# State space pipeline: four buffers for the copied C, and the spread of C as an own entry of TensorE's order

## The chip, the cores and the metric

One Trainium2 chip; the kernel runs on one of its cores. The metric is the device time of one execution in microseconds (us), taken as the median of several runs. Times inside a stage come from one profiled execution of the kernel before.

## What is computed

The program is a chain of eight residual layers on activations of 8 batches x 512 positions x 128 channels. The change touches the fifth layer alone, the state space layer. Its part of the reference, shortened:

```python
def _mamba_forward(x, W_in, conv_w, conv_b, W_x, w_dt, b_dt, A_log, D, W_out):
    xz = x @ W_in
    xc, z = jnp.split(xz, 2, axis=-1)
    ...                                     # causal convolution over 4 positions
    xs = jax.nn.silu(xconv)
    A = -jnp.exp(A_log)
    x_dbl = xs @ W_x
    Bp = x_dbl[..., 1:1 + D_STATE]
    Cp = x_dbl[..., 1 + D_STATE:]
    delta = jax.nn.softplus(d_raw * w_dt + b_dt)
    def step(h, inp):                       # over the positions
        dt, b, c, xt = inp
        At = jnp.exp(dt[..., None] * A)
        h = At * h + (dt * xt)[..., None] * b[:, None, :]
        y = jnp.einsum('bdn,bn->bd', h, c)
        return (h, y)
    ...
    y = (y + xs * D) * jax.nn.silu(z)
    return y @ W_out
```

There are 256 inner channels and 16 states (n). The layer's input is normalised first, and its output is added to the residual.

## The kernel before

The function is `mamba_all`. Channels lie on the 128 partitions in two chunks (c = 0, 1), positions run along the free dimension (512). One **step** k stands for one state n of one batch: k = 16 b + n, 128 steps in all. The recurrence over positions is one scan instruction of VectorE (DVE) per chunk, so a step is this pipeline:

- TensorE (PE) spreads row n of B over all partitions with one matmul into the PSUM bank `Bs` (L1571), and row n of C into the bank `Cs` (L1575). Both are in `spread(k)`, right behind each other. Each bank is single.
- DVE multiplies: u = dtx * Bs, both chunks in one instruction (L1384).
- ScalarE (ACT) copies `Cs` to one of the buffers `cs` (L1505) and computes the decay exp(dt * A) per chunk into the bank pair `A` (L1513).
- DVE scans per chunk: h (L1399), four buffers.
- GpSimd (POOL) weighs: hc = h * cs per chunk (L1468), six buffers.
- PE adds hc into the accumulators `Y` with an identity matmul per chunk (L1590).

The waits that matter: the copy of C for step k waits for the spread of C (`c_spread`) and for both weighings of step k - 2 (`weighed`), since `cs` has two buffers; the spread of C for step k waits until the copy of step k - 1 has read the bank (`c_taken`); the spread of B for step k waits for u of step k - 1 (`u_ready`).

```python
pe.matmul(Bs, ...).then_inc(S("b_spread"), 1)      # L1571
if k:
    pe.wait_ge(S("c_taken"), k)
pe.matmul(Cs, ...).then_inc(S("c_spread"), 1)      # L1575
```

Beside the steps of batch b, the five engines run the **batch work** of batch b + 1: normalisation (L1408 to L1523), transpose (L308), copy of it (`m_hT`, L1528), convolution and input projection (L1610, one group of four matmuls per chunk), the z part (L1616), `SiLU` on ACT (`m_xs`, `m_zs`, L1536), the projection for delta (L1621), |.| and relu on ACT (`m_mag` L1540, `m_pos` L1546), the projection to B and C (L1627), a split of them into three bf16 parts (L1553, L1421, L1561, L1562, L1442), softplus as a polynomial on DVE (L1428, L1431, L1439), dt * x on POOL (L1493). Behind a batch stand its closing pieces: D * x added (`m_yf`, L1450), the gate on POOL (L1496), the output projection (L1636) and the residual (L1455).

Every engine executes in program order. The order on an engine is made once, when the program is built: each piece of work is a Python generator that yields a due time ahead of its instructions, and `take_turns` always continues the generator whose due time is the smallest (ties go to the one listed first). Step k has the base time at(k) = 70 + 4 k, the batch work of b starts at at(16 b) - 58. These numbers set the order alone, they are no durations. Within one generator the order is that of its code, whatever due times it yields.

Of the kernel before, what the change touches and what calls it, by code (L numbers as in the profile page):

```python
# [18 lines left out]
ACT = mybir.ActivationFunctionType  # L19
AX = mybir.AxisListType  # L20

P = 128
B, T, C = 8, 512, 128
# [23 lines left out]
DI, DS, DC = 256, 16, 4  # L47
NCH = DI // P
# [106 lines left out]
def build(nc, x, pa, pb, pc, pk, pkb, b2, out):  # L155
    top = ExitStack()
    with top:
        def sb(ctx, name, shape, dt=F32):
            return ctx.enter_context(nc.sbuf_tensor(name, shape, dt))
# [1183 lines left out]
        def mamba_all(xres, wc, wconv, acoef):  # L1343
# [5 lines left out]
            with ExitStack() as ctx:  # L1349
                def room(name, shape, dt=F32):  # L1350
                    return sb(ctx, "m_" + name, shape, dt)
# [1 line left out]
                xs, zs, dt, dtx = (room(n, [P, 2, NCH, T]) for n in ("xs", "zs", "dt", "dtx"))  # L1353
                mag, pos, q = (room(n, [P, NCH, T]) for n in ("mag", "pos", "q"))
                u, h, hc = room("u", [P, 3, NCH, T]), room("h", [P, 4, T]), room("hc", [P, 6, T])
                cs, yf = room("cs", [P, 2, T]), room("yf", [P, NCH, T])
                hT, y = room("hT", [P, DC - 1 + T]), room("y", [P, NT, C])
                G, mid, rest = room("G", [96, 2, T], BF16), room("mid", [96, T], BF16), room("rest", [96, T])
                stats, mom, small = room("stats", [P, NT, 6]), room("mom", [P, 2, NT, 2]), room("small", [P, 2, 4, NT])
# [1 line left out]
                Y, Bs, Cs, A, X = flat[:, 0:2, :], flat[:, 2, :], flat[:, 3, :], flat[:, 4:6, :], flat[:, 6:8, :]  # L1361
# [3 lines left out]
                def S(name):  # L1365
                    if name not in used:
                        used[name] = pool[len(used)]
                    return used[name]

                def at(k):  # L1370
                    return 70.0 + STEP * k
# [87 lines left out]
                def gpsimd_scan(gp):  # L1459
                    for n in range(NCH * DS * B):  # L1460
                        k, c = divmod(n, NCH)
                        yield at(k) + 1.2 * (c + 2)
                        gp.wait_ge(S("scanned"), n + 1)
                        if c == 0:
                            gp.wait_ge(S("c_taken"), k + 1)
                        if n >= 6:
                            gp.wait_ge(S("summed"), n - 5)
                        gp.tensor_tensor(hc[:, n % 6, :], h[:, n % 4, :], cs[:, k % 2, :],  # L1468
                                         ALU.mult).then_inc(S("weighed"), 1)

                def gpsimd_batch(gp, b):
# [26 lines left out]
                def scalar_scan(act):  # L1498
                    for k in range(DS * B):
                        b = k // DS  # L1500
                        yield at(k) - 2.8
                        act.wait_ge(S("c_spread"), k + 1)
                        if k >= 2:
                            act.wait_ge(S("weighed"), NCH * (k - 1))
                        act.activation(cs[:, k % 2, :], Cs, ACT.Copy).then_inc(S("c_taken"), 1)  # L1505
                        for c in range(NCH):
                            yield at(k) + 1.2 * (c + 1) - 3.4
                            n = NCH * k + c
                            if k % DS == 0 and c == 0:
                                act.wait_ge(S("soft"), b + 1)  # L1510
                            if n >= 2:
                                act.wait_ge(S("scanned"), n - 1)
                            act.activation(A[:, c, :], dt[:, b % 2, c, :], ACT.Exp,  # L1513
                                           scale=acoef[:, c * DS + k % DS:c * DS + k % DS + 1]).then_inc(S("decayed"), 1)
# [47 lines left out]
                    act.activation(mid[64:96, :], rest[64:96, :], ACT.Copy).then_inc(S("mid_part"), 1)  # L1562

                def tensor_scan(pe):
                    def spread(k):
                        b, n = divmod(k, DS)
                        if n == 0:
                            pe.wait_ge(S("parted"), b + 1)
                        if k:
                            pe.wait_ge(S("u_ready"), k)  # L1570
                        pe.matmul(Bs, kb("sel32", 96)[:, n:n + 1].broadcast_to([96, P]), G[:, b % 2, :], start=True,  # L1571
                                  stop=True).then_inc(S("b_spread"), 1)
                        if k:
                            pe.wait_ge(S("c_taken"), k)
                        pe.matmul(Cs, kb("sel32", 96)[:, DS + n:DS + n + 1].broadcast_to([96, P]), G[:, b % 2, :],  # L1575
                                  start=True, stop=True).then_inc(S("c_spread"), 1)

                    for k in range(DS * B):
                        yield at(k) - 3.4
                        spread(k)  # L1580

                def tensor_sums(pe):
                    for k in range(DS * B):
# [56 lines left out]
                def all_lanes(name, eng):  # L1640
                    if name == "vector":
                        return [vector_scan(eng)] + [vector_batch(eng, b) for b in range(B)]
                    if name == "gpsimd":
                        return [gpsimd_scan(eng)] + [gpsimd_batch(eng, b) for b in range(B)]
                    if name == "scalar":
                        return [scalar_scan(eng)] + [scalar_batch(eng, b) for b in range(B)]
                    if name == "tensor":
                        return [tensor_scan(eng), tensor_sums(eng)] + [tensor_batch(eng, b) for b in range(B)]
                    return []
# [156 lines left out]
        with ExitStack() as ctx:  # L1806
# [28 lines left out]
            stage_block(load_all)  # L1835

            mamba_all(xres, wc, wc("convr"), acoef)

            with ExitStack() as inner:
# [158 lines left out]
```

## Time and profile before

| | us |
|---|---|
| median of 3 runs | 3947.56 (3946.97 to 3956.48) |
| the profiled execution, its own time | 3950.09 |
| its span in the trace | 3948.3 |
| the scan steps in it, first to last scan | 2145.7 to 2823.7 |
| granted clock of TensorE over the span, mean | 0.894 |

Times within the program are counted from the span's start. The granted clock of TensorE is given as a share of full speed: 1.00 is 2.4 GHz, 0.50 is 1.2 GHz.

### The profile page before, as it was taken

The numbers are of one execution on the slowest core, as the hardware profiler recorded it, in microseconds if no ns is written. First come the engines' busy times: TensorE is split into PE (matmuls) and PEld (weight loads), VectorE is DVE, ScalarE is ACT, GpSimd is POOL, SyncE is SP. The second block draws the span as 40 slices with busy tenths as digits, with TensorE's granted clock in tenths as the row PEclk, the third lists the DMA queues.
The fourth block names the chain that finished last, engine by engine and source line by source line (L and its number), as shares of the span: only waits on it lengthen the run. The fifth ranks groups of instructions, "written<-read, shape, count | busy, mean of one in ns | idle before, by whom it ended". The sixth has DMA issues, their size and how long they took to land. (4 is left out here: it accounts for less than half of the span.)

```text
span 3948.3 us, 49284 instructions
## 1 busy us (share of the span) xinstructions
PE 3142.3 (80%) x18104; PEld 1596.1 (40%) x18112; DVE 2337.4 (59%) x4715; ACT 1703.3 (43%) x3002; POOL 866.3 (22%) x920
## 2 busy tenths in 40 slices
PE   4988977748888397979784777767799996998977
PEld 1222224424444275656561222222377774222224
DVE  5777858856776234343423778888633234777754
ACT  1776741105556132323222454444433332576752
POOL 3222123422220000000001555555500001111001
PEclk9999987759999597989896888888899997899998
DMA  3101000001221100000002000000000000111100
GB/s 100 28 22 33 17 1 1 1 16 37 39 39 23 58 1 11 5 6 6 6 11 80 0 0 0 0 0 0 0 1 1 1 1 17 35 33 22 28 1 22
DMA packets 74519, 69.79 MB, mean 18 GB/s; under 512 B 10536, under 2 KB 72368, under 8 KB 72752
## 3 DMA queue, kind: packets, MB, share of 16 engines
q1 hardware_dynamic: 71216, 66.35, 7.3%
q8 instruction: 140, 2.29, 0.2%
q10 hardware_dynamic: 3072, 0.40, 0.1%
q14 instruction: 91, 0.75, 0.1%
HBM read 22.02 MB, written 6.29 MB: 7 GB/s over the span
## 5 line engine op out<-in xcount | busy, mean ns | idle before, releaser
L394 DVE TENSOR_REDUCE a_mx<-banks 128x1 f32<-128x512 f32 (+3 forms) x1536 | 870.7, 616 | 326.5 <-PE banks L654 200.9
L527 ACT ACTIVATE a_prob<-banks 128x512 f32<-128x512 f32 (+3 forms) x1536 | 776.0, 546 | 436.1 <-PE banks L677 206.6
L677 PE MATMUL banks<-a_Qs,a_Ks 64*128 64x512 bf16 (+3 forms) x1536 | 506.1, 363 | 108.3 <-ACT a_prob L527 101.0
L654 PE MATMUL banks<-a_Ks,a_Qs 63*128 63x512 bf16 (+3 forms) x1536 | 479.0, 370 | 28.0 <-DVE a_mx L394 15.6
L1590 PE MATMUL banks<-m_hc,kc 128*128 128x512 f32 x512 | 322.7, 735 | 124.0 <-POOL m_hc L1468 99.7
L1468 POOL TENSOR_TENSOR m_hc<-m_h,m_cs 128x512 f32<-128x512 f32 x256 | 326.6, 1294 | 305.9 <-DVE m_h L1399 305.9
L1104 ACT ACTIVATE b_room<-banks,w_b 128x512 f32<-128x512 f32 x256 | 176.0, 688 | 480.7 <-PE banks L1071 479.7
L703 PE MATMUL banks<-a_prob,a_vaug 128*32 128x512 f32 (+3 forms) x3072 | 376.3, 562 | 2.9 <-ACT a_prob L527 2.9
L1399 DVE TENSOR_TENSOR_SCAN m_h<-banks,m_u 128x512 f32<-128x512 f32 x256 | 300.7, 1207 | 27.5 <-ACT banks L1513 27.5
L654 PEld LDWEIGHTS banks<-a_Ks,a_Qs 63*128 63x128 bf16 x1536 | 130.6, 95 | 399.3 <-DVE a_mx L394 239.7
L677 PEld LDWEIGHTS banks<-a_Qs,a_Ks 64*128 64x128 bf16 x1536 | 132.2, 93 | 357.6 <-ACT a_prob L527 281.6
L1104 ACT ACTIVATE c_room<-banks 128x512 f32<-128x512 f32 x256 | 152.2, 597 | 272.9 <-PE banks L1071 272.8
L1071 PE MATMUL banks<-b_hT,w_b 128*128 128x512 f32 x512 | 256.6, 630 | 13.9 <-DMA b_x<-x 13.9
L1083 PEld LDWEIGHTS banks<-w_c,c_room 128*128 128x128 f32 x2048 | 245.6, 192 | 50.2 <-issue 50.0
L1513 ACT ACTIVATE banks<-m_dt,acoef 128x512 f32<-128x512 f32 x256 | 175.7, 690 | 196.9 <-DVE m_h L1399 192.8
L1083 PEld LDWEIGHTS banks<-w_b,b_room 128*128 128x128 f32 x2048 | 244.3, 194 | 35.0 <-issue 34.2
L1083 PE MATMUL banks<-w_c,c_room 128*128 128x128 f32 x2048 | 246.7, 275 | 0.0
L1083 PE MATMUL banks<-w_b,b_room 128*128 128x128 f32 x2048 | 246.7, 276 | 0.0
L1071 PE MATMUL banks<-c_hT,w_c 128*128 128x512 f32 x512 | 245.1, 605 | 1.2 <-ACT c_room L1104 1.2
L1384 DVE TENSOR_TENSOR m_u<-m_dtx,banks 128x1024 f32<-128x1024 f32 x128 | 154.7, 1208 | 99.4 <-PE banks L1571 96.7
L1590 PEld LDWEIGHTS banks<-m_hc,kc 128*128 128x128 f32 x512 | 96.0, 215 | 282.7 <-POOL m_hc L1468 221.5
L1118 DVE SCALAR_TENSOR_TENSOR c_room<-banks,c_room 128x128 f32<-128x128 f32 x224 | 63.0, 344 | 246.8 <-PE banks L1083 246.5
(322 smaller groups left out, 4400.9 us busy)
## 6 DMA issues: line engine op xcount, KB each, us to landing
a_Ks<-a_parts SPq DMA_DIRECT2D x288, 64.0 KB
a_Qs<-a_parts SPq DMA_DIRECT2D x288, 64.0 KB
w_c<-in_pc SPq DMA_DIRECT2D x5, 1024.0 KB
w_b<-in_pb SPq DMA_DIRECT2D x4, 1024.0 KB
a_Qs<-a_negm ACTq DMA_DIRECT2D x192, 2.0 KB
w_a<-in_pa SPq DMA_DIRECT2D x2, 1024.0 KB
xres<-in_x SPq DMA_DIRECT2D x8, 256.0 KB, 4.2
x<-xres SPq DMA_DIRECT2D x8, 256.0 KB
```

The lines of the kernel that those rows point to most:

```text
L394: dve.tensor_reduce(mx[:, g % 2, col:col + 1], M[:, k % 3, 0:keys[j]], AX.X, ALU.max).then_inc(S("max_read"), 1)
L527: act.activation(prob[:, n % 8, first_query[kt]:T], Sc[:, n % 2, first_query[kt]:T], ACT.Exp, scale=scale).then_inc(S("exped"), 1)
L654: i = pe.matmul(M[:, k % 3, 0:keys[j]], Qs[lo:lo + LAST, b % 4, pair, j * P:(j + 1) * P], Ks[lo:lo + LAST, b % 4, pair, 0:keys[j]], start= ...
L677: i = pe.matmul(Sc[:, n % 2, q0:T], Ks[lo:lo + HALF, b % 4, pair, kt * P:(kt + 1) * P], Qs[lo:lo + HALF, b % 4, pair, q0:T], start=True, s ...
L703: i = pe.matmul(V[32 * hl:32 * hl + 32, g % 2, q0:T], vaug[:, b % 3, kt, g % NG * GH + hl, :], prob[:, (4 * a + hl) % 8, q0:T], start=kt = ...
L1071: pe.matmul(bank[:, n % 2, :], w_up[:, n * P:(n + 1) * P], hT[:, :], start=True, stop=True).then_inc(S("up"), 1)
L1083: i = pe.matmul(bank[:, 2 + e % 2, j * P:(j + 1) * P], hbuf[:, n % 8, j * P:(j + 1) * P], w_down[:, n * P:(n + 1) * P], start=f == 0, stop ...
L1104: act.activation(hbuf[:, n % 8, :], bank[:, n % 2, :], func, bias=bias[:, n:n + 1] if bias is not None else 0.0).then_inc(S("acted"), 1)
L1399: dve.tensor_tensor_scan(h[:, n % 4, :], A[:, c, :], u[:, (k - 1) % 3, c, :], 0.0, ALU.mult, ALU.add).then_inc(S("scanned"), 1)
L1468: gp.tensor_tensor(hc[:, n % 6, :], h[:, n % 4, :], cs[:, k % 2, :], ALU.mult).then_inc(S("weighed"), 1)
L1513: act.activation(A[:, c, :], dt[:, b % 2, c, :], ACT.Exp, scale=acoef[:, c * DS + k % DS:c * DS + k % DS + 1]).then_inc(S("decayed"), 1)
L1590: pe.matmul(Y[:, c, :], ident, hc[:, (NCH * k + c) % 6, :], start=n == 0, stop=n == DS - 1, skip_group_check=True).then_inc(S("summed"), 1)
```

## The change

`cs` gets four buffers. The copy of C then waits for the weighings of step k - 4 in place of step k - 2. The copy's due time goes from at(k) - 2.8 to at(k) - 1.8. On TensorE the spread of B keeps at(k) - 3.4, and the spread of C gets an entry of its own at at(k) - 2.0. Lines behind this place are renumbered: the spreads are L1572 and L1577 in the changed kernel, and L1590, L1610, L1616, L1621, L1627, L1636 become L1588, L1608, L1614, L1619, L1625, L1634.

```diff
-                cs, yf = room("cs", [P, 2, T]), room("yf", [P, NCH, T])
+                cs, yf = room("cs", [P, 4, T]), room("yf", [P, NCH, T])
...
-                        gp.tensor_tensor(hc[:, n % 6, :], h[:, n % 4, :], cs[:, k % 2, :],
+                        gp.tensor_tensor(hc[:, n % 6, :], h[:, n % 4, :], cs[:, k % 4, :],
...
                 def scalar_scan(act):
                     for k in range(DS * B):
                         b = k // DS
-                        yield at(k) - 2.8
+                        yield at(k) - 1.8
                         act.wait_ge(S("c_spread"), k + 1)
-                        if k >= 2:
-                            act.wait_ge(S("weighed"), NCH * (k - 1))
-                        act.activation(cs[:, k % 2, :], Cs, ACT.Copy).then_inc(S("c_taken"), 1)
+                        if k >= 4:
+                            act.wait_ge(S("weighed"), NCH * (k - 3))
+                        act.activation(cs[:, k % 4, :], Cs, ACT.Copy).then_inc(S("c_taken"), 1)
...
                 def tensor_scan(pe):
-                    def spread(k):
+                    for k in range(DS * B):
                         b, n = divmod(k, DS)
+                        yield at(k) - 3.4
                         if n == 0:
                             pe.wait_ge(S("parted"), b + 1)
                         if k:
                             pe.wait_ge(S("u_ready"), k)
                         pe.matmul(Bs, ...).then_inc(S("b_spread"), 1)
+                        yield at(k) - 2.0
                         if k:
                             pe.wait_ge(S("c_taken"), k)
                         pe.matmul(Cs, ...).then_inc(S("c_spread"), 1)
-
-                    for k in range(DS * B):
-                        yield at(k) - 3.4
-                        spread(k)
```

What it moves. The instructions and their number are the same on every engine, and the orders of DVE and POOL are the same as before. Once per batch, seven times in all, TensorE's order changes at three places and ScalarE's at one.

The first place is on TensorE, beside the input projection of the next batch. Before (m_G is the split of B and C, m_hT the transposed input, m_hc the weighed states, m_xs the SiLU result):

```order
L1571 MATMUL banks<-m_G,kb 128x512
L1575 MATMUL banks<-m_G,kb 128x512
L1610 MATMUL banks<-m_hT,w_c 128x512 x4
L1590 MATMUL banks<-m_hc,kc 128x512 x2
L1571 MATMUL banks<-m_G,kb 128x512
L1575 MATMUL banks<-m_G,kb 128x512
L1616 MATMUL banks<-m_hT,w_c 128x512 x2
L1590 MATMUL banks<-m_hc,kc 128x512 x2
L1621 MATMUL banks<-m_xs,w_c 128x512 x2
```

The same stretch of TensorE in the changed kernel:

```order
L1572 MATMUL banks<-m_G,kb 128x512
L1608 MATMUL banks<-m_hT,w_c 128x512 x4
L1577 MATMUL banks<-m_G,kb 128x512
L1588 MATMUL banks<-m_hc,kc 128x512 x2
L1572 MATMUL banks<-m_G,kb 128x512
L1614 MATMUL banks<-m_hT,w_c 128x512
L1577 MATMUL banks<-m_G,kb 128x512
L1614 MATMUL banks<-m_hT,w_c 128x512
L1588 MATMUL banks<-m_hc,kc 128x512 x2
L1619 MATMUL banks<-m_xs,w_c 128x512 x2
```

The spread of C has moved behind the four matmuls of the second projection group, and that of the next step to between the two matmuls of the z part. In the text below the first of these steps is called s, the next s + 1, and so on.

The third place is TensorE at the output projection of the batch before (m_yf is the gated output). In the changed kernel (before, the spread of C stood ahead of the eight matmuls):

```order
L1572 MATMUL banks<-m_G,kb 128x512
L1634 MATMUL banks<-w_c,m_yf 128x128 x8
L1577 MATMUL banks<-m_G,kb 128x512
L1588 MATMUL banks<-m_hc,kc 128x512
L308 MATMUL banks<-kc,m_y 128x128 x4
```

What moved is one spread of C, behind the output projection; the work ahead of and behind it is the same.

The place on ScalarE is beside the splitting of B and C (the line with m_mag is the exponential ahead of the polynomial). One piece of the difference:

```order
 L1558 ACTIVATE banks<-m_mag 128x1024
-L1505 ACTIVATE m_cs<-banks 128x512
-L1513 ACTIVATE banks<-m_dt,acoef 128x512
 L1561 ACTIVATE m_G<-m_rest 32x512
 L1562 ACTIVATE m_mid<-m_rest 32x512
-L1513 ACTIVATE banks<-m_dt,acoef 128x512
+L1505 ACTIVATE m_cs<-banks 128x512
+L1513 ACTIVATE banks<-m_dt,acoef 128x512 x2
 L1505 ACTIVATE m_cs<-banks 128x512
```

The copy of C and the first decay have moved behind the two parts of the split. At all other places ScalarE keeps its order, the one beside SiLU too.

## Rows read from the trace of the kernel before

**Rows 1.** Busy time per engine in two stretches: us, engines, granted clock, DMA

```profile
2320.00:2410.00 90.00, 64.61 (x148) 22.35 (x146) 72.69 (x74) 44.30 (x69) 48.77 (x39) 0.87 0.00 0
2394.00:2398.00 4.00, 2.93 (x4) 0.73 (x4) 3.97 (x4) 0.86 (x2) 3.75 (x3) 0.50 0.00 0
```

**Rows 2.** Waits in the scan steps, 2140 to 2825: total us, times, longest

```profile
DVE m_u L1384 <- PE banks L1571: 96.7, 45, 4.0
ACT m_cs L1505 <- POOL m_hc L1468: 67.7, 74, 3.1
...
PE banks L1575 <- ACT m_cs L1505: 27.7, 14, 3.1
...
DVE m_h L1399 <- ACT banks L1513: 27.5, 7, 3.9
```

**Rows 3.** Timeline of a plain step: start, us, engine, line [idle before <-releaser]

```profile
2321.13 1.19 DVE L1384 TENSOR_TENSOR m_u<-m_dtx,banks 128x1024 f32<-128x1024 f32 x1
...
2322.24 2.33 DVE L1399 TENSOR_TENSOR_SCAN m_h<-banks,m_u 128x512 f32<-128x512 f32 x2
...
2322.77 0.60 ACT L1505 ACTIVATE m_cs<-banks 128x512 f32<-128x512 f32 x1 [0.83 <-POOL m_hc L1468]
...
2324.49 1.19 DVE L1384 TENSOR_TENSOR m_u<-m_dtx,banks 128x1024 f32<-128x1024 f32 x1
```

**Rows 4.** Timeline of the third batch's projection (step s and on)

```profile
2344.75 0.38 PE L1575 MATMUL banks<-m_G,kb 96*128 96x512 bf16 x1
...
2344.96 3.60 PE L1610 MATMUL banks<-m_hT,w_c 128*128 128x512 f32 x8
...
2345.16 0.60 ACT L1505 ACTIVATE m_cs<-banks 128x512 f32<-128x512 f32 x1 [3.03 <-PE banks L1575]
...
2348.40 1.88 PE L1590 MATMUL banks<-m_hc,kc 128*128 128x512 f32 x4
2348.45 0.69 ACT L1513 ACTIVATE banks<-m_dt,acoef 128x512 f32<-128x512 f32 x1 [0.42 <-DVE m_h L1399]
...
2349.16 1.28 ACT L1536 ACT_TABLE_LOAD   x1
...
2351.19 1.99 PE L1616 MATMUL banks<-m_hT,w_c 128*128 128x512 f32 x4 [0.48 <-ACT m_xs L1536]
...
2353.02 1.88 PE L1590 MATMUL banks<-m_hc,kc 128*128 128x512 f32 x4
...
2356.65 1.45 ACT L1540 ACTIVATE m_mag<-banks,w_c 128x512 f32<-128x512 f32 x2 [2.84 <-PE banks L1621]
2356.87 1.22 DVE L1384 TENSOR_TENSOR m_u<-m_dtx,banks 128x1024 f32<-128x1024 f32 x1 [2.86 <-PE banks L1571]
...
2359.98 0.39 PE L1575 MATMUL banks<-m_G,kb 96*128 96x512 bf16 x1 [3.15 <-ACT m_cs L1505]
...
2361.24 1.30 ACT L1513 ACTIVATE banks<-m_dt,acoef 128x512 f32<-128x512 f32 x2
...
2362.01 2.34 DVE L1399 TENSOR_TENSOR_SCAN m_h<-banks,m_u 128x512 f32<-128x512 f32 x2 [3.93 <-ACT banks L1513]
...
2363.64 0.38 PE L1571 MATMUL banks<-m_G,kb 96*128 96x512 bf16 x1
...
2364.27 1.19 DVE L1384 TENSOR_TENSOR m_u<-m_dtx,banks 128x1024 f32<-128x1024 f32 x1
```

**Rows 5.** Timeline: the transpose behind the output projection, a spread of B in the polynomial

```profile
2335.57 0.66 PE L308 MATMUL banks<-kc,m_y 128*128 128x128 f32 x4 [0.81 <-ACT m_y L1523]
...
2375.47 0.39 PE L1571 MATMUL banks<-m_G,kb 96*128 96x512 bf16 x1 [0.92 <-DVE m_u L1384]
```

**Rows 6.** Timeline of DVE, rows with idle time that vary between the batches

```profile
2186.07 1.22 DVE L1384 TENSOR_TENSOR m_u<-m_dtx,banks 128x1024 f32<-128x1024 f32 x1 [1.40 <-PE banks L1571]
...
2225.18 1.22 DVE L1384 TENSOR_TENSOR m_u<-m_dtx,banks 128x1024 f32<-128x1024 f32 x1 [1.17 <-PE banks L1571]
...
2314.39 1.22 DVE L1384 TENSOR_TENSOR m_u<-m_dtx,banks 128x1024 f32<-128x1024 f32 x1 [0.96 <-PE banks L1571]
...
2758.14 1.22 DVE L1384 TENSOR_TENSOR m_u<-m_dtx,banks 128x1024 f32<-128x1024 f32 x1 [0.95 <-PE banks L1571]
```

## Prediction

> **What bounds the kernel now.** I read first the busy times by stretch, then the waits, then the timeline of one batch. Over 90 us of the scan steps, about one batch, DVE is busy 72.69 us, TensorE 64.61, GpSimd 48.77 and ScalarE 44.30 [rows 1]. DVE is the engine closest to full, and it is in order, so the stage is as long as DVE's work plus DVE's idle time. Nothing in the diff changes DVE's instructions, so only its idle time counts. The waits say where that lies: 96.7 us in 45 waits of u for the spread of B, and 27.5 us in 7 waits of a scan for the decay from ScalarE [rows 2]. The wait that the four buffers aim at is another: ScalarE's copy of C waits 67.7 us in 74 waits for GpSimd's weighings [rows 2]. The question is whether any of those 67.7 us reach DVE.
>
> A plain step shows that they do not. The two u instructions start at 2321.13 and 2324.49, a step of 3.36 us; the scans start at 2322.24 and take 2.33 us, so their end, 2324.57, already overlaps the next u. DVE has no gap [rows 3]. ScalarE's copy waits 0.83 us for GpSimd in the same step, and nobody on DVE's side notices. All of DVE's idle time sits where batch work of the next batch stands in TensorE's or ScalarE's queue [rows 4].
>
> **The change part by part.**
>
> *The two more buffers.* They shorten ScalarE's waits, by up to 67.7 us in sum, in stretches where DVE is continuously busy [rows 2, 3]. The cover is DVE itself, and I cost it at 0. Were DVE faster, the step would next be bounded by the spread of B.
>
> *The spread of C behind the second projection group.* This is the term that costs. Before, the spread of C of step s starts at 2344.75 and the projection's eight passes run from 2344.96 to 2348.40, where the next matmul starts: 3.44 us. The copy of C starts 0.41 us behind the start of its spread, at 2345.16 [rows 4]. Afterwards the projection goes first: it starts at 2344.75, the spread of C at 2344.75 + 3.44 = 2348.19, the copy at 2348.19 + 0.41 = 2348.60. ScalarE is in order, and behind this copy stand both decays of step s, the load of the SiLU table, SiLU, |.| and relu, and the copy of step s + 1. The first decay starts 0.52 us behind it (0.60 for the copy, less 0.08: two decays of 0.69 take 1.30 together, so neighbours overlap by 0.08), and the two take 1.30. The table load then starts at 2348.60 + 0.52 + 1.30 = 2350.42 where it started at 2349.16 [rows 4]: **1.26 us later**. The decays themselves are still in time, for their scans run at about 2351.7.
>
> Is that delay hidden further on? TensorE waited 0.48 us for SiLU at 2351.19 already, so the z part follows SiLU and all 1.26 us go through. One more spread of C (0.22 us, the distance from 2344.75 to 2344.96) now lies between the z part's two matmuls. The z part took 1.83 us to the next start at 2353.02; four passes of 0.43 and the spread make 1.94. That adds 0.11, together **1.37 us**. The following matmuls run back to back: the sums, the projection for delta, the spread of B of step s + 2. u of that step already waited 2.86 us for it at 2356.87, so its wait becomes 4.2. Behind the same projection wait |.| (2356.65), relu, the copy of step s + 1, a table load and the decays (2361.24), and the scan at 2362.01 already waits 3.93 us for those [rows 4]. So DVE's whole position moves by 1.37 us and nothing behind it gives that back, since DVE has no more gaps until the end of the polynomial. The spread of B at 2363.64, and u at 2364.27, move along. Seven batches have this place: 7 x 1.37 = **+9.6 us**.
>
> *The spread of C behind the output projection.* TensorE then waits 0.81 us for the normalised tile before the transpose [rows 5]; a spread of 0.22 (0.43 at the lower clock) fits into that gap. ScalarE's copy stands behind the normalisation, which is later anyway. 0, at most 0.2 us per batch, 1.4 in all.
>
> *The order on ScalarE beside the split.* The copy comes about 1.3 us later (the two parts of the split are ahead of it). The spread of C behind it is later by as much, then the sums; the next spread of B waited 0.92 us for DVE at 2375.47 [rows 5], and DVE is in the polynomial with no gap. 0, with the same 0.2 per batch as upper bound.
>
> *TensorE's clock.* The granted clock is 0.50 in 2394 to 2398 and 0.87 in the mean [rows 1]. The low level reaches DVE only at a few waits: 1.40 us at 2186.07, 1.17 at 2225.18, then 0.96 once per batch, six times from 2314.39 to 2758.14 [rows 6]. That is 1.40 + 1.17 + 5.7 = 8.3 us in all. The six are 443.75 us apart over five batches, 88.75 each, to the hundredth: every batch meets the clock's changes at the same point of its work. A batch that is 1.37 us longer need not. By the trace, a batch costs 0.96 at best and 1.40 + 1.17 = 2.6 at worst; most lie at the best. I take 0.25 us more per batch, 7 x 0.25 = **+1.7 us**, nearest to the six equal rows. The ends: all of it vanishes (-8.3), or each of seven batches pays 2.6 (18.2 - 8.3 = +9.9).
>
> The Trainium skill (TensorE: Matmul & The Clock Gate, What you observe and What's actually happening) advises against fitting such ramps, as under one per cent of a span, and says that the clock's timing is free-running. By it the clock term is left out and the sum would be +9.6 in place of +11.3; the equal waits of the six batches are why I keep it.
>
> **Sum.** 0 + 9.6 + 0 + 0 + 1.7 = +11.3 us. Against the profiled execution's span that is 3948.3 + 11.3 = 3959.6, and against its own time 3950.09 + 11.3 = 3961.4. That execution lies 2.5 us above the median shown, so on the median's scale the forecast is 3947.56 + 11.3 = **3958.9 us**. This is 0.29% more; what a measurement of this kernel can tell from no change is about 0.3%, 11.8 us. The forecast is thus a small loss that just does not count.
>
> **The rivals.**
>
> *Slower, by the clock.* The delayed SiLU opens an idle gap of about 1.8 us on TensorE (0.48 before, at 2351.19) just ahead of the chain of z part, sums and projection on which DVE waits. Mechanism: the granted clock falls in this chain, or in the 3.15 us gap at 2359.98 [rows 4] as it must have done in the batch with the wait of 1.40 at 2186.07 [rows 6]. Price: 1.37 + 1.40 = 2.77 per batch if all pay, 7 x 2.77 = 19.4 us, 3967.0. It decides from two such batches in seven on (9.6 + 2 x 1.40 = 12.4). For it: the chain has no slack. Against: of seven batches with this gap one shows the wait of 1.40.
>
> *Faster, by the buffers.* TensorE's spread of C waits 27.7 us in 14 waits for the copy [rows 2]; if four buffers set the copy free, what stands behind it comes earlier, and with it B and u. All of it on the path gives 3947.56 - 27.7 = 3919.9. Against: the long one, 3.15 us, waits for a copy that stands behind |.| and relu in ScalarE's order, not behind GpSimd, and that order stays; and the u behind it does not wait (2363.64 against 2364.27 [rows 4]). The Trainium skill (Perfetto Trace Analysis, Optimization Strategy) reads gaps that repeat as a possible lack of buffers. The gaps of ScalarE's copy do repeat, but DVE, the engine that should be full, has none in those steps.
>
> *The moved spread costs nothing.* If the decays and SiLU turn out to have room that I do not see, the time stays at 3947.6. Against: two waits already name this chain, 2.86 and 3.93 us.
>
> **How the numbers follow.** The forecast gets 0.43, the costless move 0.05, so within 0.3%: 0.48. The clock rival, or any further queue effect of its sort, gets 0.44: slower. The faster case gets 0.08. The range reaches from 3948, the costless move, to 3972. The upper end is 9.6 plus the clock's upper end of 9.9 and the bounds 1.4 and 1.4 of the two small moves, 22.3 us or 3969.9, and 2 us for the scatter of the runs. Left out are the faster case and a little above.
>
> **What would show it.** In the profile of the changed kernel: the copy of C at step s starts some 3.4 us later than before, relative to its u, and the table load comes 1.3 us later. TensorE's wait for SiLU rises from 0.48 to about 1.7. DVE's wait of 2.86 becomes 4.2, and 3.93 stays as it is. ScalarE's waits for GpSimd shrink far below 67.7 without a change of the 3.36 us step. I am wrong if the step itself changes, if the waits of 2.86 stay, or if DVE's idle time grows at places that I cost at 0; the batch distance (88.75) tells the clock's share beyond 1.37.

## The result and the profile after

The changed kernel takes 3974.55 us in the median of 4 runs (3973.8 to 3976.44), the kernel before 3947.77 (4 runs, 3946.97 to 3956.48). The medians are 26.8 us apart. The ratio, which goes by the means (25.1 us apart), is 1.0064, with a 95% interval of 1.0049 to 1.0079: slower, clear of the scatter. The forecast was 3958.9 and no difference that counts; the range ended at 3972. The forecast was wrong.

The two profiled executions last 3948.3 and 3973.3 us, 25.0 apart. Where the time went is read from DVE. Its first and last row with u in the scan steps are these, in the kernel before and then in the changed one (timeline of DVE: start, us, engine, line, idle time before and its releaser):

```profile
2142.63 1.22 DVE L1384 TENSOR_TENSOR m_u<-m_dtx,banks 128x1024 f32<-128x1024 f32 x1 [2.31 <-POOL m_dtx L1493]
...
2787.73 1.22 DVE L1384 TENSOR_TENSOR m_u<-m_dtx,banks 128x1024 f32<-128x1024 f32 x1 [0.69 <-PE banks L1571]
```

```profile
2147.18 1.22 DVE L1384 TENSOR_TENSOR m_u<-m_dtx,banks 128x1024 f32<-128x1024 f32 x1 [2.31 <-POOL m_dtx L1493]
...
2816.32 1.22 DVE L1384 TENSOR_TENSOR m_u<-m_dtx,banks 128x1024 f32<-128x1024 f32 x1 [0.70 <-PE banks L1572]
```

From the first u (behind the wait for GpSimd's dt * x) to the last waiting one (0.7 us) it was 645.1 us and is 669.1, so 24.0 us more, nearly all of the 25.0. (The first start differs by 4.6 us already, in layers that the change leaves alone; runs of the kernel before scatter that much.) This stretch is the measure used below, because it leaves the other layers out.

The waits of the changed kernel, which answer to [rows 2] (waiting engine, line, engine and line waited for: total us, times, longest):

```profile
DVE m_u L1384 <- PE banks L1572: 120.2, 51, 6.0
...
ACT m_cs L1505 <- PE banks L1577: 77.3, 32, 13.1
...
PE banks L1577 <- ACT m_cs L1505: 36.6, 14, 3.1
DVE m_h L1399 <- ACT banks L1513: 27.5, 7, 3.9
```

The copy's wait for GpSimd is gone from the list; the copy now waits for the spread of C. The scans wait as before (27.5). Nearly all of the loss is in one row: u waits for the spread of B 23.5 us longer, 120.2 in place of 96.7. The timeline of one batch, which answers to [rows 4] and [rows 6], shows how (L1608 is the projection group, L1614 the z part, L1625 the projection to B and C):

```profile
2448.23 3.60 PE L1608 MATMUL banks<-m_hT,w_c 128*128 128x512 f32 x8
...
2451.67 0.38 PE L1577 MATMUL banks<-m_G,kb 96*128 96x512 bf16 x1
...
2452.09 0.60 ACT L1505 ACTIVATE m_cs<-banks 128x512 f32<-128x512 f32 x1 [6.47 <-PE banks L1577]
2452.58 1.29 ACT L1513 ACTIVATE banks<-m_dt,acoef 128x512 f32<-128x512 f32 x2
...
2453.89 1.28 ACT L1536 ACT_TABLE_LOAD   x1
...
2455.93 1.13 PE L1614 MATMUL banks<-m_hT,w_c 128*128 128x512 f32 x2 [1.94 <-ACT m_xs L1536]
...
2461.82 1.22 DVE L1384 TENSOR_TENSOR m_u<-m_dtx,banks 128x1024 f32<-128x1024 f32 x1 [4.33 <-PE banks L1572]
...
2464.93 0.39 PE L1577 MATMUL banks<-m_G,kb 96*128 96x512 bf16 x1 [3.15 <-ACT m_cs L1505]
2465.16 3.45 PE L1625 MATMUL banks<-m_xs,w_c 128*96 128x512 f32 x4
...
2466.97 2.34 DVE L1399 TENSOR_TENSOR_SCAN m_h<-banks,m_u 128x512 f32<-128x512 f32 x2 [3.92 <-ACT banks L1513]
...
2470.71 1.22 DVE L1384 TENSOR_TENSOR m_u<-m_dtx,banks 128x1024 f32<-128x1024 f32 x1 [1.40 <-PE banks L1572]
```

Two things have changed. First, the predicted chain: the projection runs first, the copy of C starts 3.44 us after it would have, the table load comes right behind the two decays, and TensorE waits 1.94 us for SiLU where it waited 0.48 (0.2 of that is only that the spread of C no longer stands ahead of the z part). u of step s + 2 waits 4.33 us in place of 2.87. Second, the four passes of L1625 behind the gap of 3.15 us take 3.45 us, and the next u waits 1.40. In the kernel before they took 1.88 in the third batch:

```profile
2360.20 1.88 PE L1627 MATMUL banks<-m_xs,w_c 128*96 128x512 f32 x4
```

The wait of 1.40 stood in one batch before, the first; it now stands in all seven.

The granted clock at this gap, in the changed kernel and then in the kernel before (busy time by stretch; the figure behind the five engines is the granted clock):

```profile
2461.80:2464.90 3.10, 0.00 (x0) 0.00 (x0) 1.22 (x1) 3.08 (x6) 0.00 (x0) 1.00 0.00 0
2464.90:2468.40 3.50, 3.47 (x5) 1.24 (x6) 1.43 (x2) 3.27 (x5) 0.13 (x1) 0.56 0.00 0
```

```profile
2356.80:2360.00 3.20, 0.05 (x2) 0.03 (x2) 1.22 (x1) 3.18 (x6) 0.00 (x0) 1.00 0.00 0
2360.00:2362.00 2.00, 2.00 (x6) 0.91 (x7) 0.00 (x0) 1.99 (x3) 0.00 (x0) 1.00 0.00 0
```

TensorE idles just as long in both, 3.15 us. Behind the gap it runs at about half clock (0.56, nearly all of the stretch at 1.2 GHz) in the changed kernel and at full clock in the kernel before. So the length of the gap alone does not decide.

A smaller part of the loss lies at the end of a batch, where u waits twice beside the output projection and the transpose. In the kernel before, once the second batch is past, the two are

```profile
2330.74 1.22 DVE L1384 TENSOR_TENSOR m_u<-m_dtx,banks 128x1024 f32<-128x1024 f32 x1 [0.45 <-PE banks L1571]
...
2337.34 1.22 DVE L1384 TENSOR_TENSOR m_u<-m_dtx,banks 128x1024 f32<-128x1024 f32 x1 [3.13 <-PE banks L1571]
```

together 3.58 us. In the changed kernel these two come to between 3.57 and 4.15 in the same batches.

### The profile page after: what moved, and what is told of

It is laid out like the page before. It is cut to its first block and busy times, and to the rows that moved or that the text cites. A ratio compares the mean times of both kernels' runs of the same rounds, so it can differ in the third digit from the quotient of the medians.

```text
span 3973.3 us, 49282 instructions
## 1 busy us (share of the span) xinstructions
PE 3162.1 (80%) x18104; PEld 1616.4 (41%) x18112; DVE 2335.7 (59%) x4715; ACT 1697.8 (43%) x3002; POOL 872.6 (22%) x920
## 5 line engine op out<-in xcount | busy, mean ns | idle before, releaser
L1588 PE MATMUL banks<-m_hc,kc 128*128 128x512 f32 x512 | 321.8, 739 | 117.9 <-POOL m_hc L1468 95.0
L1399 DVE TENSOR_TENSOR_SCAN m_h<-banks,m_u 128x512 f32<-128x512 f32 x256 | 300.8, 1207 | 27.5 <-ACT banks L1513 27.5
L1071 PE MATMUL banks<-b_hT,w_b 128*128 128x512 f32 x512 | 255.9, 628 | 13.9 <-DMA b_x<-x 13.9
L1384 DVE TENSOR_TENSOR m_u<-m_dtx,banks 128x1024 f32<-128x1024 f32 x128 | 154.9, 1210 | 122.8 <-PE banks L1572 120.2
L1588 PEld LDWEIGHTS banks<-m_hc,kc 128*128 128x128 f32 x512 | 102.8, 223 | 275.2 <-POOL m_hc L1468 199.3
```

Of the source, the lines that this page charges most:

```text
L1071: pe.matmul(bank[:, n % 2, :], w_up[:, n * P:(n + 1) * P], hT[:, :], start=True, stop=True).then_inc(S("up"), 1)
L1399: dve.tensor_tensor_scan(h[:, n % 4, :], A[:, c, :], u[:, (k - 1) % 3, c, :], 0.0, ALU.mult, ALU.add).then_inc(S("scanned"), 1)
L1588: pe.matmul(Y[:, c, :], ident, hc[:, (NCH * k + c) % 6, :], start=n == 0, stop=n == DS - 1, skip_group_check=True).then_inc(S("summed"), 1)
```

## The experiments

All ratios are to the kernel before, run on the same chip beside each kernel. In the experiments that kernel's median was 3954 to 3955.5 us, so ratios are compared and not times. The stretch is first to last u, as above, from each kernel's profiled execution; "direct" is seven times what the edit adds to a batch by its own rows, and "rest" what is left. Stretch and rest come from one execution each. The three kernels that should not differ in them (before, four buffers, moved behind the output projection) lie within 0.4 us.

| kernel | ratio (95%) | stretch, us | against 645.1 | direct | rest |
|---|---|---|---|---|---|
| the change | 1.0064 (1.0049 to 1.0079) | 669.1 | +24.0 | 7 x 1.46 = 10.2 | 13.8 |
| four buffers alone | 0.9999 (0.999 to 1.0009) | 645.0 | -0.1 | 0 | 0 |
| moved behind the output projection alone | 0.9991 (0.9982 to 1.0001) | 645.4 | +0.3 | 0 | 0.3 |
| first move alone | 1.0057 (1.004 to 1.0075) | 669.9 | +24.8 | 7 x 1.24 = 8.7 | 16.1 |
| second move alone | 1.0017 (1.0006 to 1.0027) | 652.1 | +7.0 | 7 x 0.22 = 1.5 | 5.5 |
| the change, gap filled | 1.0045 (1.0028 to 1.0061) | 665.8 | +20.7 | 10.2 | 10.5 |
| before, padded by 1.11 | 1.0038 (1.0024 to 1.0052) | 659.0 | +13.9 | 7 x 1.11 = 7.8 | 6.1 |
| before, padded by 3.11 | 1.0054 (1.0034 to 1.0075) | 668.8 | +23.7 | 7 x 3.11 = 21.8 | 1.9 |
| before, copy first | 0.993 (0.9914 to 0.9947) | 621.1 | -24.0 | -7 x 3.53 = -24.7 | 0.7 |
| the change, copy first | 0.9973 (0.9963 to 0.9983) | 635.1 | -10.0 | -24.7 + 10.2 = -14.5 | 4.5 |
| before, batch work spread out | 0.9918 (0.9902 to 0.9935) | 621.3 | -23.8 | | |
| spread out further | 0.9935 (0.9916 to 0.9954) | 621.4 | -23.7 | | |

The theory to be tested (A) was: the order of TensorE costs the time, through the one spread of C behind the second projection group, and a clock share comes on top. The rivals were the buffers, and the other two places.

**Four buffers alone.** The diff's lines on `cs` and on the copy's wait, with all due times and `spread(k)` as before.

```diff
-                cs, yf = room("cs", [P, 2, T]), ...
+                cs, yf = room("cs", [P, 4, T]), ...
-                        if k >= 2:
-                            act.wait_ge(S("weighed"), NCH * (k - 1))
+                        if k >= 4:
+                            act.wait_ge(S("weighed"), NCH * (k - 3))
```

> Four buffers of the copied C alone, with the order on every engine as before. Theory A (the order of TensorE costs the time, the buffers are idle): the time of before, 3947.8 us within 0.3%, ScalarE's waits of the copy for GpSimd well below 67.7 us, DVE's waits for the spread of B near 96.7. Rival B (the buffers let the copy run ahead and shift the engines against each other, or their memory costs): a good part of the 26.8 us, 3960 or more.

Ratio 0.9999. Its waits of the copy:

```profile
ACT m_cs L1505 <- POOL m_hc L1468: 0.7, 1, 0.7
```

```profile
DVE m_u L1384 <- PE banks L1571: 96.4, 45, 3.9
```

The wait that the buffers aim at falls from 67.7 us [rows 2] to 0.7, and DVE's waits do not move: 96.4 us, as before. The buffers neither help nor hurt.

**Only behind the output projection.** The whole change with another due time for the spread of C:

```diff
-                        yield at(k) - 2.0
+                        yield at(k) - 2.6
```

> The whole change, but the spread of C is due 0.6 earlier (at(k) - 2.6). It then keeps its old place beside the projection and the z part, and has moved only behind the output projection; ScalarE's order beside the split is that of the change. Theory A (the place beside the projection costs): 3947.8 to 3951 us, u waits of 2.87 and not 4.33, at most one wait of 1.40. Rival C (the output projection or the split costs, which I had put at 0): 3955 or more.

Ratio 0.9991, DVE's waits 96.8 and 27.5 us. The move behind the output projection, and ScalarE's new order beside the split, are free together, as costed.

**First move alone.** Step s is n = 5 of the batch that is being scanned.

```diff
-                        yield at(k) - 2.0
+                        yield at(k) - (2.0 if n == 5 else 3.4)
```

The copy's due time is at(k) - 2.8 again in this kernel and the next.

> Only the one spread of C of step s is moved behind the second projection group, once per batch; all other places of TensorE and ScalarE as before, four buffers. Theory A (this move delays SiLU by 1.26 us, the gap in front of the z part shifts TensorE against its clock): about the time of the change, 3970 to 3976, with u waits of 4.2 to 4.3 in the chain and the wait of 1.40 in most batches. Plain sum without the clock: 7 x 1.26 = 8.8, so 3956.6. Rival: the cost is the spread between the z part's matmuls: 3948.

Ratio 1.0057, the whole loss within the intervals. Timeline of DVE, two rows of one batch:

```profile
2460.16 1.22 DVE L1384 TENSOR_TENSOR m_u<-m_dtx,banks 128x1024 f32<-128x1024 f32 x1 [4.11 <-PE banks L1572]
...
2469.04 1.22 DVE L1384 TENSOR_TENSOR m_u<-m_dtx,banks 128x1024 f32<-128x1024 f32 x1 [1.40 <-PE banks L1572]
```

The wait is 4.11 where 2.87 + 1.26 = 4.13 was worked out, in all seven batches, and behind the gap 1.40 stands in six batches and 2.64 in the first.

**Second move alone.** The same with `n == 6`.

> Only the spread of C of step s + 1 is moved to between the two matmuls of the z part; all else as before, four buffers. Theory A: 0.1 to 0.2 us per batch, 3948 to 3950, no wait of 1.40 beyond the one in the first batch. Rival (this one spread is what hurts): 3960 or more.

The chain wait is 3.09 us in every batch, 0.22 more than before: one spread, 1.5 us in seven batches, as worked out. But the ratio is 1.0017 and the stretch 7.0 us longer, so the rest is 5.5 us. Both expectations, the time and no wait of 1.40 beyond the first batch, are missed. The rows show where most of the rest is: behind the gap of 3.15 us nothing is lost in the second and the third batch, and then a wait of 1.40 appears in the fourth and one of 2.49 in the fifth.

```profile
2460.57 1.22 DVE L1384 TENSOR_TENSOR m_u<-m_dtx,banks 128x1024 f32<-128x1024 f32 x1 [1.40 <-PE banks L1572]
...
2552.98 1.22 DVE L1384 TENSOR_TENSOR m_u<-m_dtx,banks 128x1024 f32<-128x1024 f32 x1 [2.49 <-PE banks L1572]
```

TensorE's rows at this gap in the third and the fifth batch:

```profile
2366.00 0.39 PE L1577 MATMUL banks<-m_G,kb 96*128 96x512 bf16 x1 [3.15 <-ACT m_cs L1505]
2366.22 1.88 PE L1625 MATMUL banks<-m_xs,w_c 128*96 128x512 f32 x4
...
2546.12 0.61 PE L1577 MATMUL banks<-m_G,kb 96*128 96x512 bf16 x1 [3.15 <-ACT m_cs L1505]
2546.52 3.62 PE L1625 MATMUL banks<-m_xs,w_c 128*96 128x512 f32 x4
```

Busy time by stretch behind the gap, third, fourth and fifth batch (granted clock behind the five engines):

```profile
2366.00:2369.60 3.60, 3.60 (x9) 1.52 (x10) 1.57 (x2) 3.37 (x5) 0.26 (x1) 1.00 0.00 0
2454.80:2458.40 3.60, 3.60 (x7) 1.61 (x8) 1.57 (x2) 3.37 (x5) 0.27 (x1) 0.69 0.00 0
2546.10:2549.70 3.60, 3.58 (x5) 1.45 (x6) 1.54 (x2) 3.37 (x5) 0.24 (x1) 0.50 0.00 0
```

One kernel, one order and one length of gap, and the granted clock behind it is 1.00, 0.69 and 0.50. An edit that adds 0.22 us to a batch cannot itself add 2.49. What is left to differ, as far as these rows show, is when a batch meets the clock's changes. That led to theory L: batches can settle in step with the clock's changes, and what makes a batch longer takes them out of step, whatever it is.

**The gap filled.** The change, with the four passes of the projection to B and C ahead of the waiting spread of C:

```diff
-                    yield t + 20.0
+                    yield t + 19.0
                     pe.wait_ge(S("silu"), 4 * b + 4)
```

> The whole change, with the projection to B and C (four passes, 1.7 us) taken ahead of the spread of C of step s + 2 on TensorE, into the gap in which that spread waits for the copy (3.15 us). The delayed SiLU stays (u wait of 4.33). Theory A with the clock (the wait of 1.40 behind the gap is TensorE at half clock, entered because the gap is met at the wrong moment): the seven waits of 1.40 vanish, DVE's idle falls by about 9.7 us, and the time is 10 to 14 us below that of the change, 3961 to 3965 where before is 3948 (ratio to before 1.003 to 1.0045). Rival (the 1.40 is not the clock's but the order's): as the change, ratio 1.006 or more, u waits of 1.40 kept or moved one step on.

Half a hit. All seven waits of 1.40 are gone and TensorE's gap is 1.4 us, yet DVE's waits for B fall only from 120.2 to 117.6, not by 9.7. The ratio is 1.0045, the upper end of the expected range. Rows from the third and the sixth batch:

```profile
2356.38 1.22 DVE L1384 TENSOR_TENSOR m_u<-m_dtx,banks 128x1024 f32<-128x1024 f32 x1 [5.24 <-PE banks L1572]
...
2369.77 1.22 DVE L1384 TENSOR_TENSOR m_u<-m_dtx,banks 128x1024 f32<-128x1024 f32 x1 [4.33 <-PE banks L1572]
...
2614.28 1.22 DVE L1384 TENSOR_TENSOR m_u<-m_dtx,banks 128x1024 f32<-128x1024 f32 x1 [1.01 <-PE banks L1572]
...
2621.81 1.22 DVE L1384 TENSOR_TENSOR m_u<-m_dtx,banks 128x1024 f32<-128x1024 f32 x1 [4.07 <-PE banks L1572]
```

The wait at the first projection group, 3.54 in the kernel before, is 5.24 in this one batch of the seven: 1.7 us. The wait of 6.02 in the first batch (4.33 in the others) is another 1.7. Most of the rest of 10.5 us lies in the two waits beside the output projection and the transpose: together they reach 5.08 us (1.01 and 4.07) where 3.58 stood, and over the stretch they sum to 32.3 us, 7.2 more than before. The rival, that the 1.40 keeps its place by the order, falls; but filling the gap saves only 3.3 us of the stretch, so the gap is not the whole cause either. It is one of the places where the cost can land.

**A pad on DVE.** The kernel before with an instruction that nobody reads, once per batch for b > 0, ahead of the polynomial:

```diff
+                            if b:
+                                if b > 1:
+                                    dve.wait_ge(S("pads"), b - 1)
+                                dve.tensor_scalar(pad[:, :, :], X[:, :, :], factor, None, ALU.mult).then_inc(S("pads"), 1)
                             i = dve.tensor_scalar(q[:, :, :], X[:, :, :], factor, None, ALU.mult)
```

> The kernel before with one more DVE instruction of about 1.2 us per batch (seven in all) ahead of the polynomial, its result unused; all queues as before. Plain sum: 7 x 1.2 = 8.4 us, ratio 1.0021, all chain waits as before (2.87, 3.93). Theory L (a longer batch falls out of step with the changes of TensorE's clock, whatever makes it longer): batches no longer 88.75 us apart, waits of 1.40 in several batches, 12 to 24 us in all, ratio 1.003 to 1.006. If the 1.40 stays out, the gap in front of the z part is what brings it.

Neither TensorE's nor ScalarE's order is touched. The pad takes 1.11 us from its start to the next:

```profile
2382.67 1.20 DVE L1432 TENSOR_SCALAR m_pad<-banks 128x1024 f32<-128x1024 f32 x1
2383.78 1.21 DVE L1433 TENSOR_SCALAR m_q<-banks 128x1024 f32<-128x1024 f32 x1
```

Seven pads are 7.8 us, and the stretch is 13.9 longer: a rest of 6.1. Theory L had expected waits of 1.40 in several batches. They did not come: the 1.40 stays a thing of the first batch. The rest sits at another place, in four batches at the first projection group:

```profile
2355.78 1.22 DVE L1385 TENSOR_TENSOR m_u<-m_dtx,banks 128x1024 f32<-128x1024 f32 x1 [5.24 <-PE banks L1576]
```

The projection itself is slow there (TensorE's own timeline, eight passes in 5.37 us, 3.60 at full clock), in a stretch with a granted clock of 0.78:

```profile
2348.44 5.37 PE L1615 MATMUL banks<-m_hT,w_c 128*128 128x512 f32 x8 [1.79 <-DVE xres_c L1460]
```

```profile
2348.00:2355.80 7.80, 7.36 (x15) 3.17 (x16) 2.56 (x4) 1.38 (x2) 2.49 (x2) 0.78 0.01 2
```

So a longer batch can cost TensorE's clock without any change in TensorE's or ScalarE's queue. Why the loss lands here and not behind the gap was not worked out.

**A pad in step.** Three such instructions, the third a narrower one, 3.11 us together (2291.85 to 2294.96 in its trace):

```profile
2291.85 3.20 DVE L1434 TENSOR_SCALAR m_pad<-banks 128x1024 f32<-128x1024 f32 x3
2294.96 1.21 DVE L1435 TENSOR_SCALAR m_q<-banks 128x1024 f32<-128x1024 f32 x1
```

> The kernel before with three more DVE instructions per batch (seven batches), two of 1.2 us and one of about 1.0, together about 3.4 us, results unused. Theory L (batches settle at distances that are in step with the clock's changes; seen so far are 85.4, 88.75 and 92.15 us, 3.4 apart): the batch distance becomes 92.15, no wait of 1.40 behind the first batch, chain waits as before, first to last u longer by the plain 7 x 3.4 = 23.9 us and at most 2 us more, ratio 1.006. So this kernel, padded by three times as much as the one with 1.2, has less of the clock's extra cost than its 5.5 us. Rival (every lengthening costs its extra, growing with the pad): 30 us or more, ratio 1.0075 or more, waits of 1.40 or 5.24 in most batches.

As theory L has it, and against the rival: nearly three times the pad, but a rest of 1.9 us in place of 6.1, no wait of 5.24, and no 1.40 behind the first batch. Its waits for s + 2 lie at 2276.9, 2369.0, 2461.12, 2553.23, so these batches are 92.1 us apart (the last two distances are 92.5 and 92.0). By the ratios alone the rests are 2 to 13 us for the short pad and -8 to 8 for the long one; these overlap, so that the two pads differ rests on the rows of one execution each. Two of the waits:

```profile
2461.12 1.22 DVE L1385 TENSOR_TENSOR m_u<-m_dtx,banks 128x1024 f32<-128x1024 f32 x1 [2.87 <-PE banks L1578]
...
2553.23 1.22 DVE L1385 TENSOR_TENSOR m_u<-m_dtx,banks 128x1024 f32<-128x1024 f32 x1 [2.86 <-PE banks L1578]
```

**Copy first.** The kernel before with ScalarE's abs and relu behind the copy and the decays of step s + 1:

```diff
-                    yield t + 15.0
+                    yield t + 17.5
                     act.wait_ge(S("dt_projected"), b + 1)
```

> The kernel before, with ScalarE's abs and relu moved behind the copy of C and the two decays of step s + 1 (they stood ahead of them). Two buffers, TensorE's order as before. Theory A (DVE's 3.93 us and TensorE's 3.15 us in each batch wait for that copy and those decays only because abs and relu stand ahead): the scan wait of 3.93 falls to 0 to 0.5, a wait for B of about 0.4 comes behind it, 7 x 3.5 = 24 us less, ratio 0.9935 to 0.9945 if the clock plays along. Rival (abs and relu are late instead and delay the polynomial): ratio 0.998 or more.

A hit by the stretch, 24.0 us less; the ratio of 0.993 is a little below the expected range, which its interval covers. One batch in its timeline:

```profile
2439.47 1.22 DVE L1384 TENSOR_TENSOR m_u<-m_dtx,banks 128x1024 f32<-128x1024 f32 x1 [2.87 <-PE banks L1571]
2440.60 2.33 DVE L1399 TENSOR_TENSOR_SCAN m_h<-banks,m_u 128x512 f32<-128x512 f32 x2
...
2443.33 1.22 DVE L1384 TENSOR_TENSOR m_u<-m_dtx,banks 128x1024 f32<-128x1024 f32 x1 [0.40 <-PE banks L1571]
```

The scan follows u without a wait (3.93 before), 0.40 comes behind it. Batches are 85.4 us apart (2354.1, 2439.47, 2524.83), and the rest is 0.7. By theory L this shorter batch is in step too.

**The change, copy first.** The same line moved in the changed kernel.

> The whole change, and abs and relu on ScalarE behind the copy of C and the decays of step s + 1. Theory A: the scan wait of 3.93 and TensorE's wait of 3.15 vanish as they did without the change, the delayed SiLU stays (u wait of 4.33), so it lies 10 us plus a clock share of 0 to 14 above the same move without the change (ratio there 0.993): ratio 0.9955 to 0.999. Rival (with this order the spread of C behind the projection costs nothing): ratio 0.993.

Ratio 0.9973, in the range of theory A. The wait of 4.33 stays. The change still costs 14.0 us on top of the better order (635.1 against 621.1): 10.2 direct and 3.8 more, put down to the clock by subtraction.

**Batch work spread out.** The kernel before; the projection in four pairs of matmuls, the transpose behind the spreads, all from SiLU on two steps later:

```diff
-                        if c:
-                            yield t + 11.5
                         for d in range(DC):
+                            if d == 0 and c or d == 2:
+                                yield t + 7.2 + 8.0 * c + (4.0 if d else 0.0)
...
-                    yield t + 5.0
+                    yield t + 7.5
                     pe.wait_ge(S("normed"), b + 1)
...
-                    yield t + 15.0
+                    yield t + 22.9
                     if b >= 2:
                         act.wait_ge(S("gated"), b - 1)
```

> The kernel before, with the batch work spread over more steps: the eight projection matmuls in four pairs, one per step, SiLU and all behind it two steps later, the transpose behind the spreads instead of ahead of them, abs and relu behind copy and decays. Theory A (all of DVE's idle time, 17 us per batch, comes from batch work that stands in lumps ahead of spreads of B): DVE's waits fall from about 17 to 5 to 9 us per batch, 55 to 85 us less, ratio 0.979 to 0.986. Rival (the later polynomial makes the next batch wait for dt and its product, or GpSimd's normalisation stays the limit): under 30 us less.

A miss by size: 23.8 us less in the stretch where 55 to 85 were expected, within the rival's "under 30". The pairs work: where 3.54 and 2.12 us were lost, four waits of 0.40 to 1.83 stand. But a lump remains, the z part and the projection for delta ahead of one spread of B, now behind a TensorE that has waited for SiLU: 4.58 us, and 6.28 in some batches. Ratio 0.9918; the interval overlaps with that of the single moved line, which this edit contains. (The profiled execution of this kernel took 3935.3 us, its median is 3924.8, so its stretch may be on the long side.)

**Spread out further.** Delta's projection behind the next spread of B, that to B and C one step later (due t + 26.7 and t + 30.7).

> The kernel with the batch work spread over more steps, and the projections for delta and for B and C each one entry later, behind the spread of B instead of ahead of it. Theory A (what stands ahead of a spread of B is what DVE waits for): its wait of 4.58 falls by the 1.7 us of the four passes, and one wait of 0.4 may come behind it, 7 x 1.3 to 1.7 = 9 to 12 us less than without it: ratio 0.988 to 0.990. Rival (SiLU's table load and the z part set this step, or the clock takes it back): 0.9918 as before.

A miss: the ratio is not below that of the kernel it builds on. One batch:

```profile
2524.30 1.22 DVE L1384 TENSOR_TENSOR m_u<-m_dtx,banks 128x1024 f32<-128x1024 f32 x1 [2.86 <-PE banks L1571]
2528.18 1.22 DVE L1384 TENSOR_TENSOR m_u<-m_dtx,banks 128x1024 f32<-128x1024 f32 x1 [0.29 <-PE banks L1571]
2530.19 2.34 DVE L1399 TENSOR_TENSOR_SCAN m_h<-banks,m_u 128x512 f32<-128x512 f32 x2 [0.79 <-ACT banks L1513]
2533.65 1.22 DVE L1384 TENSOR_TENSOR m_u<-m_dtx,banks 128x1024 f32<-128x1024 f32 x1 [1.13 <-PE banks L1571]
```

The wait of 4.58 falls by the 1.7 as expected, to 2.86, but 0.29, 0.79 and 1.13 stand behind it: ScalarE's abs and relu now wait for a later projection, and the decays behind them are late. The stretch, 621.4 us, is no shorter.

## Why the prediction was wrong

- *The buffers at 0*: right, shown alone (0.9999). The Trainium skill (Perfetto Trace Analysis, Optimization Strategy) reads repeating gaps on the engine that should be full as a possible lack of buffers; the gaps here were on ScalarE, and taking 67 us of them away gave nothing.
- *The spread of C behind the projection, +1.26*: right. u waits 4.11 in the kernel with that move alone, 2.87 + 1.24. *One more spread in the z part, +0.11*: it cost 0.22, the full spread; the two matmuls did not absorb any of it. Together 1.46 per batch, 10.2 us, where +9.6 was forecast.
- *Output projection and split at 0*: right (0.9991).
- *TensorE's clock, +1.7*: this is the step that failed. The rest beyond the direct cost is 13.8 us, above even the upper end of +9.9. I had seen that six batches lie 88.75 us apart to the hundredth, and said that a longer batch need not meet the clock at the same point, but then priced it by those six batches, that is by the state which the change ends. By the rows of the changed kernel the 13.8 are: the wait of 1.40 in six more batches, 8.4; the wait of the first batch, 6.03 in place of 4.33, where TensorE ran the second half of the z part and most of the sums behind it at about half clock (granted 0.53 from 2178.4 to 2181.8), 1.7; the two waits beside the output projection and the transpose, 2.3; the wait that was 0.96 and is now 1.01 to 1.17, 0.8; and 0.6 outside these waits. My worst case of 2.6 per batch counted only the first and the last kind of wait; the other two I took for nothing. In other kernels the projection at half clock (5.24 in place of 3.54) was a further place that it left out.
- *The rival "slower, by the clock"*: it is what happened, including the wait of 1.40 in all seven batches. Its price of 19.4 us was below the 24.0 of the stretch. Its mechanism was half right: a kernel whose gap ahead of the z part is as short as it was (the pad of 1.11 us on DVE) pays too, so the larger gap is not needed for a cost of the clock. What the kernels that pay have in common is a batch of another length; that a length alone decides is not shown.
- *Faster by the buffers*: falls. The long wait of TensorE for the copy (3.15) has nothing to do with GpSimd: with four buffers alone it stayed, and it fell to 0.8 when abs and relu were moved behind the copy.

Of the 25.0 us between the two profiled executions 24.0 lie in the stretch; 10.2 are the queue, 13.8 are put down to the clock by subtraction. The other 1.0, and the 1.8 by which the medians differ more, are within the scatter of the runs.

What stays open: why the clock share is 13.8 with both moves, 16.1 with one, 5.5 with the other and 1.9 with the long pad was not worked out. That the low clock causes the long passes is read from the granted clock beside them (0.56, 0.78, and 1.00, 0.69, 0.50 in one kernel); no run held the clock fixed. Theory L is supported by these rows and by the two pads, but not proved: it named in advance that the short pad would cost extra and the long one would not, and it did not name the place where the short pad's cost landed.

## What to carry to other kernels

In a pipeline with in-order queues, a buffer helps only if the waiting engine's delay reaches the engine without gaps; follow what stands *behind* the instruction that waits, on its own queue, and move that. Splitting a helper into two entries of a planner's order looks free, but the second entry falls behind other work at the few places where lumps stand, and whoever copies its result is then late with all that is queued behind. And when a repeated block with TensorE work in it gets longer or shorter, allow for a share of TensorE's clock that can be larger than the direct cost of the edit (here from 1.9 us beside 21.8 to 5.5 us beside 1.5), and measure it: a pad on another engine tells it apart from the queues.

## What the runs showed of the hardware

Three kernels repeat at a nearly fixed distance, two of them with a small rest in the table beside the kernel before: 88.75 us before, 85.4 with the shorter chain, 92.1 with the long pad. In the changed kernel the waits of 1.40 lie at 2378.9, 2470.7, 2563.2, 2655.0 and 2747.5, alternately 91.8 and 92.5 apart, 92.15 in the mean; so a distance near 92.1 does not by itself mean a small clock share. Not every kernel settles: the one spread out further has 85.1 five times and then 86.1, and the change with copy first varies from 86.3 to 88.7. A pad of 1.11 us on an engine that is not TensorE cost 1.98 us per batch (13.9 / 7), one of 3.11 us cost 3.39 (23.7 / 7). The same eight passes took 3.60 us at the full clock and 5.37 where the granted clock was 0.78 over the stretch. The same idle gap of 3.15 us was followed by the full clock, by 0.69 and by 0.50 in three batches of one kernel. The Trainium skill (TensorE: Matmul & The Clock Gate, What's actually happening) prices the ramp at under one per cent of a typical kernel's span. What this change adds stays below that, 13.8 of 3948 us being 0.35%; but it is more than the direct cost of the edit.
